# Attention and two-way expert layer on one core: first stack loads issued later, the order of the attention steps changed, the last division cut in four

## The reference

```python
qkv = x @ W_attn.T + b_attn                       # x: (4, 1024, 256)
att = einsum('bhqd,bhkd->bhqk', q, k) / sqrt(16) + rel_bias   # 32 buckets of distance
att = softmax(where(causal, att, -inf))
x = layernorm(x + (att @ v) @ W_proj.T + b_proj)
top1 = argmax(x @ gate_w.T)                       # 2 experts
routing = sum_e(relu(masked_e @ w1[e] + b1[e]) @ w2[e] + b2[e])   # 256 -> 1024 -> 256
shared  = relu(x @ sw1 + sb1) @ sw2 + sb2
out = layernorm(x + routing + shared)
```

## Time and profile before

| | before |
|---|---|
| median of 3 runs | 833.5 us (833.4 to 835.99) |
| profiled execution | 833.7 us, of which its span 832.0 us |
| PE busy | 777.1 us (93%) |
| weight loads (PEld) | 556.8 us (67%) |
| DVE busy | 514.6 us (62%) |
| ACT busy | 542.7 us (65%) |
| POOL busy | 243.5 us (29%) |
| granted PE clock, mean | 0.976 |

### The profile page before, as it was taken

The page is one execution under the profiler, slowest core; times in us unless marked ns, Lnnn a source line. Parts: engine busy times, 40 slices in busy tenths (PEclk is TensorE's granted clock), DMA queues, the critical chain, the costliest instruction groups (busy, mean ns, idle before and its releaser), DMA issues.

```text
span 832.0 us, 15414 instructions
## 1 busy us (share of the span) xinstructions
PE 777.1 (93%) x5761; PEld 556.8 (67%) x5761; DVE 514.6 (62%) x1120; ACT 542.7 (65%) x698; POOL 243.5 (29%) x199
## 2 busy tenths in 40 slices
PE   7994879999999999999979999999999999999993
PEld 6884633333334333343869988989899989999993
DVE  4662556666676666766886887886735445544453
ACT  5552659999999999999435556543444555555552
POOL 6221510000020021036154453443433232233332
PEclk9997979999999999999989999999999999999997
DMA  8899975577796699791582111201285334444300
GB/s 233 230 278 217 212 233 91 92 114 117 127 183 115 118 171 159 135 170 20 105 274 64 65 52 59 71 26 53 86 304 197 121 130 168 170 178 163 140 26 29
DMA packets 57878, 114.33 MB, mean 137 GB/s; under 512 B 7971, under 2 KB 35016, under 8 KB 55496
## 3 DMA queue, kind: packets, MB, share of 16 engines
q1 hardware_dynamic: 53000, 100.57, 51.0%
q0 software_dynamic: 4800, 12.73, 4.4%
HBM read 57.75 MB, written 32.46 MB: 108 GB/s over the span
## 4 chain that ended last, share of the span: by engine, by line
PE 74%; DVE 10%; ACT 7%; issue 4%; DMA 3%; POOL 1%; SPq 0%; POOLq 0%; DVEq 0%; ACTq 0%
PE slots L2027 19%; PE o_ps L1170 12%; PE slots L1151 11%; PE slots L2044 10%; PE o_ps L2044 10%; PE slots L701 4%; ACT probs L1059 4%; DVE slots L1117 3%; PE slots L1392 2%; ACT probs L1061 2%; DMA x_in<-L_attn_x 2%; PE o_ps L663 2%; DVE junk L1784 2%; PE slots L644 1%; DMA qk_d<-parts 1%
## 5 line engine op out<-in xcount | busy, mean ns | idle before, releaser
L1059 ACT ACTIVATE probs<-slots 128x1024 f32<-128x1024 f32 x252 | 237.6, 1037 | 5.6 <-DVE slots L1117 4.8
L1117 DVE TENSOR_TENSOR slots<-slots,bias_t 128x512 f32<-128x512 f32 (+1 forms) x288 | 160.3, 605 | 83.8 <-PE slots L1151 82.9
L1935 DVE TENSOR_TENSOR h_lo<-h_f,h_hi 128x512 fp32r<-128x512 f32 (+1 forms) x136 | 95.9, 706 | 106.5 <-PE o_ps L2044 62.4
L1170 PE MATMUL o_ps<-probs,v_st 128*32 128x512 f32 (+3 forms) x1664 | 154.6, 472 | 1.8 <-ACT probs L1059 0.4
L1753 ACT ACTIVATE h_f<-slots,b_cur 128x512 f32<-128x512 f32 (+1 forms) x72 | 47.9, 665 | 88.0 <-PE slots L2027 81.9
L1753 ACT ACTIVATE h_f<-slots,b_c 128x512 f32<-128x512 f32 x64 | 44.0, 687 | 73.6 <-PE slots L2027 65.4
L1757 ACT ACTIVATE h_hi<-h_f 128x512 fp32r<-128x512 f32 (+1 forms) x136 | 84.3, 620 | 4.3
L1151 PEld LDWEIGHTS slots<-q_first,k_st 50*128 50x128 f32 x416 | 34.7, 188 | 65.6 <-ACT probs L1059 43.5
L1151 PE MATMUL slots<-q_first,k_st 50*128 50x512 f32 (+3 forms) x416 | 69.0, 399 | 7.7 <-ACT probs L1059 2.7
L1151 PEld LDWEIGHTS slots<-q_second,k_st 50*128 50x128 f32 x416 | 34.0, 184 | 62.1 <-ACT probs L1059 44.4
L1170 PEld LDWEIGHTS o_ps<-probs,v_st 128*32 128x32 f32 x1664 | 39.9, 109 | 49.5 <-issue 30.2
(11 more groups left out here) (240 smaller groups left out, 1744.5 us busy)
## 6 DMA issues: line engine op xcount, KB each, us to landing
qk_d<-parts SPq DMA_DIRECT2D x32, 512.0 KB, 8.3
cur_hi<-experts_hi SPq DMA_DIRECT2D x9, 1024.0 KB, 4.8
cur_lo<-experts_lo SPq DMA_DIRECT2D x9, 1024.0 KB, 7.1
k_st<-qk_d SPq DMA_DIRECT2D x32, 256.0 KB
xs_sb<-xs_d SPq DMA_DIRECT2D x8, 528.0 KB, 4.6
x_in<-L_attn_x SPq DMA_DIRECT2D x8, 512.0 KB, 8.4
k_st<-qk_d SPq DMA_DIRECT2D x32, 128.0 KB
q_first<-qk_d SPq DMA_DIRECT2D x16, 256.0 KB
```

The costliest lines, as they stand in the source:

```text
L1059: nc.scalar.activation(dst, src, ACT.Exp).then_inc(exped, 1)
L1117: ins = dve.tensor_tensor(tile, tile, bias_t[:, h0:h0 + 2, first:first + w], ALU.add)
L1170: ins = pe.matmul(o_ps[32 * j2:32 * j2 + 2 * D, half, q:q + w], v_st[:, g, j, j2, :], probs[:, (k + j2 // 2) % PBUFS, j2 % 2, col:col + w] ...
L1935: dve.tensor_tensor(h_lo[:, n % 3, 0:w], h_f[:, q % 2, 0:w], h_hi[:, n % 3, 0:w].bitcast(F32), ALU.subtract).then_inc(hl_ok, 1)
```

## The change

Three edits. `first_stack(0)` is issued between `body(2)` and `body(3)` and waits for the stores of three batches; `first_stack(1)` is issued after the four guard DMAs, in front of the last tile's stores, and waits for nothing of its own. The steps of a unit are in another order, and two whole blocks are cut: key blocks 1 and 2 against half 1 are now `LONG` (queries 0 to 383) and `SHORT` (the last 128). The nine steps become (1,3), (0,0), (0,3 and long 1,1), (0,2 and left 1,0), (0,1 and short 1,1), (1,4), (1,6 and right 1,0), (1,5 and short 1,2), (1,7 and long 1,2); DVE's share of them is 256, 512, 256, 512, 512, 512, 512, 512, 256. `EVAC0` moves from step 8 to step 7. The division of the last batch is four instructions of 512 elements instead of one of 2048, and the one consumer waits for all four.

```diff
-STEPS = [[WHOLE[1][1]], [WHOLE[1][3]], [WHOLE[1][2]]] + [[x] for x in WHOLE[0]]
-STEPS += [[WIDE[0], NARROW[0]], [WIDE[1], NARROW[1]]]
-STEPS += [[MIDDLE[0], FAR_LEFT], [WHOLE[1][4]], [MIDDLE[1], FAR_RIGHT]]
+LONG, SHORT = ([(1, j, q, w, q) for j in (1, 2)] for q, w in ((0, TT - P), (TT - P, P)))
+STEPS = [[WHOLE[1][3]]] + [[x] for x in WHOLE[0]] + [[NARROW[0], LONG[0]], [MIDDLE[0], FAR_LEFT], [WIDE[0], SHORT[0]]]
+STEPS += [[WHOLE[1][4]], [MIDDLE[1], FAR_RIGHT], [WIDE[1], SHORT[1]], [NARROW[1], LONG[1]]]
...
-            def first_stack(g, b):
-
-                for t in range(TPB):
-                    sp.wait_ge(stored[t], 16 * NC * b)
-                if g == 0:
-                    sp.wait_ge(pool_set, 4)
-                    sp.wait_ge(guard_out, 16)
+            def first_stack(g):
+
                 q_st = (q_first, q_second)[g]
                 load_parts(sp, *unit_rows(qk_d, 0, g), k_st[:, g], q_st, st_ld[g])
                 load_guard(sp, guard_d, 0, g, q_st, st_ld[g])
 
-            body(0, False, True)
-            body(1, True, True)
-            first_stack(0, 2)
-            body(2, True, True)
-            first_stack(1, 3)
+            for b in range(B - 1):
+                body(b, b > 0, True)
+            for t in range(TPB):
+                sp.wait_ge(stored[t], 16 * NC * (B - 1))
+            sp.wait_ge(pool_set, 4)
+            sp.wait_ge(guard_out, 16)
+            first_stack(0)
             body(B - 1, True, False)
...
+            first_stack(1)
             sp.wait_ge(ready.decided, 1)
             store_tile(B - 1, TPB - 1)
...
-        EVAC1, EVAC0, INVERT = (1, 1), (NSTEP - 1, 1), (0, 1)
+        EVAC1, EVAC0, INVERT = (1, 1), (NSTEP - 2, 1), (0, 1)
...
-        y = y_t[:, :, bass.ds(b * T, T)]
-        pool.tensor_tensor(y, y, rs_row[:, :, :], ALU.mult).then_inc(step.y_norm, 1)
+        if b < B - 1:
+            y = y_t[:, :, bass.ds(b * T, T)]
+            pool.tensor_tensor(y, y, rs_row[:, :, :], ALU.mult).then_inc(step.y_norm, 1)
+            return
+        for t in range(TPB):
+            for kc in range(KC):
+                y = y_t[:, kc, bass.ds(b * T + TT * t, TT)]
+                ins = pool.tensor_tensor(y, y, rs_row[:, kc, TT * t:TT * t + TT], ALU.mult)
+                ins.then_inc(step.y_norm, 1)
...
-            act.wait_ge(divide.y_norm, B + 1)
+            act.wait_ge(divide.y_norm, B + TPB * KC)
```

## The result

The changed kernel takes 819.4 us (median of 4 executions, 817.1 to 823.5) against 833.5 before: a ratio of 0.983, interval 0.981 to 0.985. Run again it took 818.4 (6 executions, 816.1 to 824.1), a ratio of 0.984 (0.980 to 0.987). The prediction was 817.7. The two together show which terms hold each time and which do not.

The account below looks back on a forecast made before the run. Bounds: a late load in the projection, an ACT-PE-DVE loop in the attention, PE's wait behind DVE in feed-forward. From 833.7 us, -12.6 + 1.4 - 4.6 + 0 gave 817.9, set at 817.7; range 812 to 823.

Parts of the forecast that it names:

- Stacks: Projection: moving the first_stack calls frees the loads of tiles 6 and 7; 13.05 us less 0.5 for lateness, gain 12.6.
- Start: Start of the attention: the first exponential must now wait for DVE's first addition; loss 1.4 us.
- the prediction's upper case: Start of the attention: with the same 1.7 us of stalls as before, exponential 8 comes 2.0 later.
- Rival (c): Start of the attention stays at half clock for another ten us; 4 more, 821.6 us; chance 0.12.
- Steady state: Attention units: the new step order shortens DVE's delays of ACT; 0.33 us for each of 14 units, gain 4.6.
- The walk: Attention unit priced step by step: last six steps 11.24 us where before stood 11.57, the three ahead 5.78.
- Rival (b): Attention: PE's cut steps, three in a row twice a unit, eat the steady gain; 822.2 us; chance 0.13.
- Pieces: Division of the last batch in four instructions: taken as 0, bounds 0.5 us gain and 1 loss.
- rival (a): First feed-forward tile: the division pieces let DVE through; up to 7.4 us less, 810.2; chance 0.12.
- DVE waits for nothing there: Attention: EVAC0's copy, a step earlier, meets outputs finished two steps before, so it costs no wait.
- (d): Projection: the queue is too full, tiles 6 and 7 and tile 5's buffer late by 2 us each; 823.5; chance 0.05.
- (e): Attention: every step waits for DVE, 4.11 us for two steps; 18.4 more, 840.9 us; chance 0.03.

Follow-up runs that it names:

- e_again: The changed kernel once more, unaltered; median 818.4 us, ratio 0.984 to the kernel before.
- e_xfirst: The kernel before with only tile 6's load moved ahead of first_stack(0, 2); 834.8 us, ratio 1.000.
- e_evac: The changed kernel with EVAC0 back at the last step of a unit; 819.1 us, ratio 0.983 to before.
- e_late: The changed kernel with the four division pieces moved behind the scatters of the second tile; 820.0 us, ratio 0.986 to before.
- e_steps: The kernel before with only the new step order and EVAC0 place; 833.4 us, ratio 1.000.
- e_stacks: The kernel before with only the two first_stack calls moved; 822.4 us, ratio 0.986.
- e_far2: The changed kernel with a whole first step that needs no bias and key blocks 2 and 3 cut; 820.7 us, ratio 0.984 to before.
- e_quiet: The kernel of e_late with both loads of shared weights moved to the last batch; 817.5 us, ratio 0.981 to before.
- e_steps2: The same kernel as e_steps, run again for another profile; 832.1 us, ratio 0.997 to before.
- e_far: The changed kernel with a first step that needs no bias and only key block 2 cut; 824.8 us, ratio 0.990 to before.
- e_both: The kernel of e_far2 with the division late as in e_late; 818.1 us, ratio 0.981 to before.

## Why the prediction came out right, and where it did not

The time was right, and the sum behind it is close: -12.6 + 1.4 - 4.6 + 0 = -15.8 foretold, -15.9 in the spans of before and e_again (831.97 to 816.03), -10.3 in the first profile. That the sum meets e_again's within 0.1 is partly luck: by stretch it is -13.15 + 2.8 - 4.9 - 0.7, so 1.4 too little at the start is made up by 0.55, 0.3 and 0.7 elsewhere. By the table's columns, changed kernel less before:

**Stacks, right.** Predicted 13.05 less 0.5, counted from the chain's 90.44; the first of tile 7's transposes starts at 90.28. Measured 12.65 and 13.15 at tile 7, 12.4 with the stacks alone. Tile 7's load was to land at 76.9 and landed at 77.6. `first_stack(0)` was issued at 82.6 (82.1 predicted). e_xfirst shows that the second half of the argument, the 12.1 us that a stack takes of the queue, is needed: moving the load alone leaves the whole loss in place.

**Start, the term that was mis-sized.** Predicted 1.4, bounds 0.3 and 2.0. The step order alone cost 2.1 and 3.2; the whole change 2.8 in e_again, 3.2 and 3.3 in e_evac and e_late, and 5.2 in the first profile. The stalls behind exponential 0 were what the prediction's upper case says, "with the same 1.7 of stalls as before", 9.7 us from exponential 0 to 8: measured 9.7 to 10.1 in six of the seven profiles with the new first step, 10.5 in the first one. What was mis-sized is the step from there to 1.4. It took off 0.6 because part of the stalls "lies under exponentials that now come later", and none did: 2.0 was the better term. On top of that exponential 0 itself was late. It was foretold 24.6 behind tile 7's transposes (114.85 less 90.28) and came at 24.4 in e_steps and 25.4 to 25.9 in the other six. In five of these six the projection's end is later by 1.4 to 1.6, with the half clock just behind tile 7, which e_stacks and e_far2 have too, so that part is not the step order's; in e_again it is later by 0.3, and the other 0.5 is not explained.

Rival (c), a longer half clock at the start of the attention, came in part: 13.7 us in e_again, e_steps and e_quiet and 17.1 in the first profile, but 10.2 as before in e_steps2, e_evac and e_late. It was priced at 4. From exponential 0 to the second unit the first profile took 21.5 and the other six 19.7 to 20.1, so even its 17.1 cost 1.5 to 1.9.

**Steady state, right, in size and in mechanism.** 17.36 to 17.03 is the 0.33 predicted, in every execution profiled, and the stretch to the last exponential is 4.9 shorter. The walk gave the last six steps of a unit as 1.83, 1.96, 1.83, 1.96, 1.83 and 1.83, 11.24 together, and 5.78 for the three ahead of them. Measured are 1.83, 1.96, 1.82, 1.97, 1.83 and 1.81, 11.22 together, and 5.81. The loop from exponential to exponential takes 3.8 for two steps and no longer 4.11, and e_far and e_far2 show that the gain goes with the steps of 768 elements. Rival (b), that PE's cut steps eat the gain, did not come: six of nine steps are cut, and two of them took PE no more than 1.83 (0.79 or 0.83 of scores, 1.00 of outputs), under the 1.86 that the prediction gave them. The other four took up to 2.0, with the wait for ACT in it. How much PE alone could save beyond this was not tried.

**Pieces, right.** Predicted 0; 0.3 of PE's wait, 0.8 (2.2 to -0.5) in time. Each `junk` ran beside one piece, as argued, so rival (a) had nothing to gain.

**Not foreseen: stalls at batch boundaries.** In three of the eight profiles of kernels with units of 17.0 to 17.1 and the shared loads in place (the changed one, e_far2, e_both) the first unit of a batch that follows a load of shared weights waits 2 to 10 us, twice by the trace's own account for the sums DMA. None was seen in the five profiles with units of 17.36. It was counted as "DVE waits for nothing there". Shown are the waits, what for in two of them, and that the shared load ahead of each took at least 4 us longer to land than any other. Argued only is that units 0.33 shorter leave a late queue less time, and that the shared load is what makes it late. The DMA share speaks neither for nor against it: from 140 to 375 us it is 0.79 before and 0.79 in e_again. Whether these stalls are also what e_steps lost in its times of 837 to 842 stays open: no profile fell on one of those.

Rivals (d) and (e) did not happen: tiles 6 and 7 were late by 0 and 0.3, and no ordinary unit ran at 4.11 for two steps.

## What to carry to other kernels

Before a load is taken out from behind a burst of DMAs, ask what stands behind the burst next: moving the burst to where no load follows saved 12 us, and moving one load ahead of it, with the next one still behind, saved nothing. When two engines look full, don't take the larger share of the chain, or a time from start to start, for the bound: PE's steps of 2.0 us held a wait for ACT, and ACT's gaps ended with DVE's additions. Compare the start of an instruction with the end of what it needs. And judge a kernel whose executions differ by more than the edit is worth from stretches of several profiles, not from one span.

## What the runs showed of the hardware that was not expected

POOL and DVE do not always take turns. In front of four `junk`, each division piece let one through. At the late place the same four pieces ran back to back in 5.04 us, and DVE's `picked`, four elements per partition, took 4.58 us and ended with the last of them. Why it got no gap between pieces was not tried. The Trainium skill, SBUF — State Buffer, section Who interferes with whom, has the pair of ports held for a whole instruction by whoever issued first; it says so where it speaks of DVE's two-port modes, and of an instruction with two inputs in SBUF only that it contends with GpSimd's reads. If the one that waits came next, `picked` would have waited for one piece of 1.3 at most; here it waited for all four, and the page does not say who follows.

Issuing a DMA is not always 0.5 us: behind a stack's ten DMAs two bias DMAs took 5.11 and one load 5.33 (e_xfirst), and with no stack ahead the changed kernel's load at 63.41 took 2.16 and the store behind it 3.14. SP can do nothing else meanwhile, and everything in its order is later. That a full queue is the reason is likely but was not tried.

A wait of PE costs more than its length, but not always: in e_far2 two waits of 3.9 and 3.2 us were followed by ten at a granted clock of 0.52, 1.2 instead of 2.4 GHz for nearly all of it, and the two units lost 9.7 together. Behind the same wait of 2.89 for `h_lo` the clock fell for 6.8 us in e_both and not at all in e_late and e_quiet.
